# Two phases instead of one pipeline: the first product for every row and a store, then neighbour sums by accumulating gathers

## What is computed

```python
x = x + _L0_gnn_ref(_layernorm(x), edge_index, W, b)
x = x + _L0_ffn_ref(_layernorm(x)[None], ...)[0]
# _L0_gnn_ref, self edges added to the list (row, col):
h = jnp.einsum('nd,od->no', x, W) + b
deg = jnp.zeros((num_nodes,)).at[row].add(1.0)
deg_inv_sqrt = deg ** (-0.5)
norm = deg_inv_sqrt[row] * deg_inv_sqrt[col]
out = jax.ops.segment_sum(norm[:, None] * h[col], row, num_segments=num_nodes)
# _L0_ffn_ref: base product + shared rank 16 + 6 routed experts of rank 16, the best 2 weighted by a softmax
base_out = jnp.einsum('bsi,oi->bso', x, base_W) + base_b
```

## Time and profile before

| what | value |
|---|---|
| median of 3 runs | 2338.88 us (2337.76 to 2340.23) |
| span of the profiled execution | 2337.9 us |
| TensorE (PE) busy | 2259.6 us, 97% |
| VectorE (DVE) busy | 1602.0 us, 69% |
| ScalarE (ACT) busy | 399.7 us, 17% |
| GpSimd (POOL) busy | 410.7 us, 18% |
| moved by DMA | 113.56 MB, mean 49 GB/s |

### The profile page before, as it was taken

The page is one execution under the profiler, slowest core; times in us unless marked ns, Lnnn a source line. Parts: engine busy times, 40 slices in busy tenths (PEclk is TensorE's granted clock), DMA queues, the critical chain, the costliest instruction groups (busy, mean ns, idle before and its releaser), DMA issues.

```text
span 2337.9 us, 35957 instructions
## 1 busy us (share of the span) xinstructions
PE 2259.6 (97%) x12190; PEld 2060.8 (88%) x12190; DVE 1602.0 (69%) x4079; ACT 399.7 (17%) x808; POOL 410.7 (18%) x666
## 2 busy tenths in 40 slices
PE   3499999999999999999999999999999999999999
PEld 2389999999999999999999999999999999999998
DVE  8676676667667666667667766766666666676673
ACT  3011111121111111111111111111111111111110
POOL 9311111111111111111111111111111111111110
PEclk7699999999999999999999999999999999999999
DMA  4011111111111111111111111111111111111110
GB/s 188 17 44 46 44 47 50 43 44 45 47 51 53 46 45 45 44 45 46 54 45 45 45 46 49 51 46 44 45 44 44 44 55 46 46 45 44 48 38 27
DMA packets 39747, 113.56 MB, mean 49 GB/s; under 512 B 12138, under 2 KB 12217, under 8 KB 39730
## 3 DMA queue, kind: packets, MB, share of 16 engines
q1 hardware_dynamic: 25826, 92.79, 10.8%
q0 software_dynamic: 13904, 20.55, 3.3%
HBM read 92.78 MB, written 41.46 MB: 57 GB/s over the span
## 4 chain that ended last, share of the span: by engine, by line
PE 96%; DVE 3%; DMA 0%; issue 0%; ACT 0%; POOL 0%; POOLq 0%; SPq 0%; DVEq 0%
PE bo L616 15%; PE bo L618 14%; PE bo L617 14%; PE bg L616 13%; PE bg L618 13%; PE bg L617 13%; PE bt L625 6%; PE bo L698 2%; PE bo L702 2%; PE bo L700 2%; PE bt L663 2%; PE bt L664 2%; DVE slot_vals L770 1%; PE bm L665 0%; PE bm L691 0%; DVE hot_local L730 0%
## 5 line engine op out<-in xcount | busy, mean ns | idle before, releaser
L616 PE MATMUL bo<-base_hi,z_hi 128*128 128x380 f32 (+1 forms) x1896 | 659.3, 348 | 1.6 <-DVE z_lo L911 1.6
L618 PE MATMUL bo<-base_hi,z_lo 128*128 128x380 f32 (+1 forms) x1896 | 637.4, 336 | 0.0
L617 PE MATMUL bo<-base_lo,z_hi 128*128 128x380 f32 (+1 forms) x1896 | 635.9, 335 | 0.0
L616 PE MATMUL bg<-w_hi,u_hi 128*128 128x512 f32 x1264 | 507.1, 401 | 3.5 <-issue 2.0
L618 PE MATMUL bg<-w_hi,u_lo 128*128 128x512 f32 x1264 | 500.1, 396 | 0.0
L617 PE MATMUL bg<-w_lo,u_hi 128*128 128x512 f32 x1264 | 500.0, 396 | 0.0
L616 PEld LDWEIGHTS bo<-base_hi,z_hi 128*128 128x128 f32 x1896 | 357.5, 189 | 1.9 <-ACT z_hi L529 1.8
L617 PEld LDWEIGHTS bo<-base_lo,z_hi 128*128 128x128 f32 x1896 | 358.1, 189 | 0.0
L618 PEld LDWEIGHTS bo<-base_hi,z_lo 128*128 128x128 f32 x1896 | 356.0, 188 | 0.0
L922 DVE TENSOR_TENSOR y<-bo,y 128x262 f32<-128x262 f32 (+2 forms) x237 | 119.5, 513 | 320.6 <-PE bo L702 312.9
L467 POOL TENSOR_TENSOR pw<-pin,neg_half 128x4 f32<-128x4 f32 x79 | 80.6, 1021 | 1361.4 <-DVE pin L883 1337.8
(11 more groups left out here) (136 smaller groups left out, 2596.9 us busy)
## 6 DMA issues: line engine op xcount, KB each, us to landing
xb<-x SPq DMA_DIRECT2D x79, 512.0 KB, 4.4
out<-y SPq DMA_DIRECT2D x79, 512.0 KB, 2.6
base_raw<-base_t SPq DMA_DIRECT2D x8, 571.0 KB, 16.2
w_raw<-w_t SPq DMA_DIRECT2D x8, 512.0 KB, 6.8
xg<-x,row_now POOLq DMA_INDIRECT x79, 4.3
pin<-deg,row_now POOLq DMA_INDIRECT x79, 4.0
b_rows<-b SPq DMA_DIRECT2D x1, 512.0 KB, 11.4
bl_raw<-b_low SPq DMA_DIRECT2D x1, 452.0 KB
```

What stands on the lines that cost most here:

```text
L616: nc.tensor.matmul(ps, hi[:, k, :], m_hi[:, k, n], start=(k == 0), stop=False)
L617: nc.tensor.matmul(ps, hi[:, k, :], m_lo[:, k, n], start=False, stop=False)
L618: last = nc.tensor.matmul(ps, lo[:, k, :], m_hi[:, k, n], start=False, stop=(ends and k == KB - 1))
```

## The change

The kernel is cut into two phases, with a barrier between them.

Phase one, 79 steps written out without a loop: a tile of x is loaded (five buffers), normalised (`un`), transposed, multiplied by W (three pairs of banks), weighted by the node's deg^-0.5 on ScalarE (`weigh`), and b is added (`finish_rows`), which gives h; r = x * deg^0.5 + h. SP stores h and r to DRAM, 512 KB each. Nothing of the neighbours is needed here. Beside it, the edge tables are made: the one-hot tables in step 1 (`degrees`), 40 small products for the degrees in tile 2's product, the two powers for all 79 tiles at once on GpSimd in step 2, and in 28 of the steps from 6 on the rank of each edge among those of the same source (`compare`, up to 30 chunks of 128 comparisons in a step). From step 42 on GpSimd scatters the edges' targets into a slot table in DRAM, four slots for each node, which comes back in step 51. The dense layer's weights are loaded and split in steps 52 to 61, over the space of these tables. VectorE makes the low parts of the weights, where GpSimd did.

Between the phases GpSimd waits for every store of h and r and reads the overflow flag (a node with more than four outgoing edges); SP's loads of phase two wait for its signal.

Phase two, a loop of six steps a turn: SP loads a tile of r into one of six buffers `acc`; GpSimd adds to it, in four rounds, the rows h of the targets in slot 0, 1, 2 and 3, each by an indirect DMA that gathers and adds (`add_edges`). An empty slot points at one of 128 zero rows behind h, so every round moves 128 rows. The sum is the node's new row but for a factor deg^-0.5. VectorE takes its statistics (`acc_statistics`), ScalarE makes z, and the second product follows as before, with two sets of three banks. `finish` scales the sum and adds the product, and SP stores it. The gathered rows' normalisation, their split and the `sel` products are gone.

```diff
+ROUNDS = 4
+LANE_SLOTS = TILES * ROUNDS
+SLOTS = P * LANE_SLOTS
+DEEP = 6
+COMPARED = 30
+RANK_AT, SCATTER_AT, BASE_AT = 6, 42, 52
...
+                if s.has(-1):
+                    t = s.tile(-1)
+                    a = s.mod(-1, DEEP)
+                    sp.wait_ge(out_ok, 3 * (t + 1))
+                    sp.dma_start(out[rows(t), :], acc[a][:]).then_inc(out_stored[a], 16)
+                if s.has(5):
+                    a = s.mod(5, DEEP)
+                    if s.has(-1):
+                        sp.wait_ge(out_stored[a], 16 * (s.uses(5, DEEP) - 1))
+                    sp.dma_start(acc[a][:], r_dram[rows(s.tile(5)), :]).then_inc(r_in[a], 16)
+            sp.wait_ge(rows_ready, 1)
+            pipeline(sp, step, -5, TILES, 5)
...
+            def rstd(t):
+                pool.wait_ge(stats_ok, t + 1)
+                nc.gpsimd.tensor_tensor(pw[:], pin[:], neg_half[:, 0:1], ALU.pow) \
+                    .then_inc(rstd_ok, 1)
+            rstd(0)
+            rstd(1)
+            for t in range(TILES):
+                if t == 2:
+                    pool.wait_ge(deg_ok, 1)
+                    nc.gpsimd.tensor_tensor(dis[:], deg[:], neg_half[:], ALU.pow).then_inc(dis_ok, 1)
+                    nc.gpsimd.tensor_tensor(sqd[:], deg[:], pos_half[:], ALU.pow).then_inc(dis_ok, 1)
+                if t + 2 < TILES:
+                    rstd(t + 2)
...
+            def add_edges(a, q, r):
+                nc.gpsimd.indirect_dma_start(
+                    acc[a][:], None, h_dram,
+                    bass.IndirectOffsetOnAxis(ap=row_now[q][:, r:r + 1], axis=0),
+                    bounds_check=NPAD + P - 1, oob_is_err=True, compute_op=ALU.add) \
+                    .then_inc(added[r], 16)
             def step(s):
...
+                if s.has(4):
+                    t = s.tile(4)
+                    nc.gpsimd.tensor_copy(row_now[s.mod(4, 2)][:],
+                                          offs[:, bass.ds(t * ROUNDS, ROUNDS)]) \
+                        .then_inc(row_copied, 1)
+                    pool.wait_ge(row_copied, t + 1)
+                    pool.wait_ge(r_in[s.mod(4, DEEP)], 16 * s.uses(4, DEEP))
+                    carry_wait(4 + 4 * (s.q % 2))
+                    add_edges(s.mod(4, DEEP), s.mod(4, 2), 0)
+                if s.has(3):
+                    pool.wait_ge(added[1], 16 * (s.tile(3) + 1))
+                    carry_wait(5 + 4 * (s.q % 2))
+                    add_edges(s.mod(3, DEEP), s.mod(3, 2), 2)
                 if s.has(2):
...
+                    pool.wait_ge(acc_stats_ok, s.tile(2) + 1)
+                    nc.gpsimd.tensor_tensor(pw[:], pin[:], neg_half[:, 0:1], ALU.pow) \
+                        .then_inc(acc_rstd_ok, 1)
+                if s.has(4):
+                    pool.wait_ge(added[0], 16 * (s.tile(4) + 1))
+                    carry_wait(6 + 4 * (s.q % 2))
+                    add_edges(s.mod(4, DEEP), s.mod(4, 2), 1)
+                if s.has(3):
+                    pool.wait_ge(added[2], 16 * (s.tile(3) + 1))
+                    carry_wait(7 + 4 * (s.q % 2))
+                    add_edges(s.mod(3, DEEP), s.mod(3, 2), 3)
+                    pool.wait_ge(added[3], 16 * (s.tile(3) + 1))
+            pipeline(pool, step, -4, TILES - 3, 5)
...
+            def weigh(t):
+                if t == 0:
+                    act.wait_ge(dis_ok, 1)
+                if t >= 2:
+                    act.wait_ge(h_stored[t % 2], 16 * (t // 2))
+                    act.wait_ge(r_ok, t - 1)
+                for h in range(2):
+                    act.wait_ge(first_done, 2 * t + h + 1)
+                    nc.scalar.activation(hrow[t % 2][:, h * HALF:(h + 1) * HALF],
+                                         bg[t % 3][h][:], ACT.Copy, scale=dis[:, t:t + 1]) \
+                        .then_inc(h0_ok, 1)
...
+            for t in range(1, TILES):
+                pe.wait_ge(u_hi_ok, 2 * (t + 1))
+                pe.wait_ge(u_lo_ok, 2 * (t + 1))
+                for h in range(2):
+                    if t >= 3:
+                        pe.wait_ge(h0_ok, 2 * (t - 3) + h + 1)
+                    for k in range(KB):
+                        last = passes(bg[t % 3][h][:], u_hi[t % 2], u_lo[t % 2], w_hi, w_lo,
+                                      slice(h * HALF, (h + 1) * HALF), k, True)
+                    last.then_inc(first_done, 1)
+                    if h == 0 and t == 2:
+                        pe.wait_ge(hot_ok, 2)
+                        for c in range(CHUNKS):
+                            last = nc.tensor.matmul(bt[0][:, 0:TILES], hot_local[:, c, :],
+                                                    hot_tile[:, c, :], start=(c == 0),
+                                                    stop=(c == CHUNKS - 1))
+                        last.then_inc(deg_done, 1)
+                    if h == 0 and t + 1 < TILES:
+                        transpose_rows(t + 1)
...
-                    for h in range(2):
-                        half = slice(h * HALF, (h + 1) * HALF)
-                        nc.tensor.matmul(bt[h][:], sel[:], g_hi[:, half], start=True, stop=False)
-                        nc.tensor.matmul(bt[h][:], sel[:], g_lo[:, half], start=False, stop=True)
-                    nc.tensor.matmul(bm[:, HALF - 2:HALF - 1], sel[:].bitcast(F32), pw[:, 3:4],
-                                     start=True, stop=True).then_inc(sum_done, 1)
...
+            def finish_rows(t):
+                if t == 0:
+                    dve.wait_ge(rows_in, 32)
+                    dve.wait_ge(dis_ok, 2)
+                dve.wait_ge(h0_ok, 2 * (t + 1))
+                nc.vector.scalar_tensor_tensor(hrow[t % 2][:], b_rows[:], dis[:, t:t + 1],
+                                               hrow[t % 2][:], ALU.mult, ALU.add).then_inc(h_ok, 1)
+                dve.wait_ge(h_ok, t + 1)
+                nc.vector.scalar_tensor_tensor(xn[t % 5][:], xn[t % 5][:], sqd[:, t:t + 1],
+                                               hrow[t % 2][:], ALU.mult, ALU.add).then_inc(r_ok, 1)
...
+            def compare(pieces):
+                every = src_row[:].rearrange("q (p c) -> q c p", c=CHUNKS)
+                for c, a, to, where in pieces:
+                    first = CHUNKS - c + a
+                    link(nc.vector.scalar_tensor_tensor(
+                        same_src[:, 0:to - a, :], every[:, a:to, :], srcs[:, c:c + 1],
+                        earlier_of[:, first:first + to - a, :], ALU.is_equal, ALU.mult,
+                        accum_out=rank_parts[:, where, c:c + 1]))
...
+            for t in range(TILES + 1):
+                if t >= 3:
+                    finish_rows(t - 1)
+                if t + 2 < TILES and t != 2:
+                    statistics(t + 2)
+                if t == 1:
+                    degrees()
+                if t == 2:
+                    dve.wait_ge(deg_done, 1)
+                    nc.vector.tensor_scalar(deg[:], bt[0][:, 0:TILES], 1.0, None, ALU.add) \
+                        .then_inc(deg_ok, 1)
+                    dve.wait_ge(deg_ok, 1)
+                    link(nc.vector.reciprocal(dis2[:], deg[:]))
+                if t + 1 < TILES:
+                    low_rows(t + 1)
+                if t == 2:
+                    statistics(4)
+                if t + 2 < TILES:
+                    scales(t + 2)
+                if t == 2:
+                    finish_rows(0)
+                    finish_rows(1)
+                if t == RANK_AT - 1:
+                    columns()
+                if RANK_AT <= t < RANK_AT + len(PIECES):
+                    compare(PIECES[t - RANK_AT])
...
+            def acc_statistics(s):
+                n = s.tile(2)
+                a = acc[s.mod(2, DEEP)]
+                accs.start(n)
+                dve.wait_ge(added[3], 16 * (n + 1))
...
             def step(s):
-                if s.has(-2):
+                if s.has(-1):
                     finish(s)
-                if s.has(1):
-                    prepare_scales(s)
-                if s.has(-1):
-                    low_parts(s, -1, z_hi, z_lo, z_hi_ok, z_lo_ok)
-                if s.has(1):
-                    prepare_low(s)
+                if s.has(2):
+                    acc_statistics(s)
                 if s.has(0):
-                    dve.wait_ge(xb_ok, s.tile(0) + 1)
-                    make_y(s)
-                if s.has(1):
-                    if not s.has(0):
-                        dve.wait_ge(rows_in, 32)
-                    add_sum(s)
-                if s.has(0):
-                    make_z(s)
-                if s.has(-1):
                     choose(s)
                 if s.has(1):
-                    low_parts(s, 1, u_hi, u_lo, u_hi_ok, u_lo_ok)
-                if s.has(-1):
-                    p = s.tile(-1)
+                    low_parts(s)
+                if s.has(0):
+                    p = s.tile(0)
                     dve.wait_ge(hs_hi_ok, p + 1)
```

(89 more changed lines are left out.)

1038 lines of the change are left out of this document (472 added, 566 removed).

## The result

The change makes the kernel slower: 2623.38 us, median of 4 runs (2621.30 to 2625.43), against 2339.53 us for the kernel before on the same chip (4 runs, 2337.76 to 2340.23). The ratio is 1.122, 95% interval 1.120 to 1.123. The forecast was 2248 us, on the other side; the time lies at the upper end of the range, in the case called much slower gathers.

The account below looks back on a forecast made before the run. TensorE was taken to bound the kernel: 1000 for phase one, 51 between the phases, 2 for the clock, 79 x 15.06 (1190) for phase two and 4 at the end, 2247 us of span, 2248 us as median; range 2225 to 2635.

Parts of the forecast that it names:

- much slower gathers: Phase two: the chain of adding gathers sets the pace at 18 to 22 us a tile, 2480 to 2790 us; chance 0.27.
- The beginning: Start of phase one: constants, hot tables and powers delay TensorE; tile 4 starts at 96 us, 48 us late.
- one idle stretch of 15 us: Phase one, tile 3: TensorE idle behind GpSimd's two powers of 79 columns, named as a sign.
- a rival that came true: Phase one's 28 rank steps: VectorE bounds them, strided reads at slot_vals' rate, 36 us lost, 2284 us; within the 0.45.
- Between the phases: From phase one's end to TensorE's restart: 51 us with gathers of 4.5 us, 59 with 5.6, plus 2 for the clock.
- T = 3.95 + 2L: Phase two: time per tile of GpSimd's gather chain, with two landings L; TensorE's 15.06 us cover it up to L = 5.55.
- middle case: Phase two: adding costs one more read of 512 KB, L = 5.65, 15.3 us a tile, about 16.5 with collisions.
- The sign that I had named above all: Phase two: a landing of the gathers over 6 us would show the prediction wrong.
- my own sum: Whole kernel if gathers set the pace: 1000 + 37 first tile + 78 T + 38 last, so 1075 + 78 T.
- The two cases with slow gathers: Phase two paced by the gather chain: somewhat slower, 2290 to 2450 us, chance 0.28; much slower, 2480 to 2790, 0.27.
- the third: Phase two: TensorE stays the bound at 15.06 us a tile, 2248 us, own range 2225 to 2310; chance 0.45.
- the upper bound of L: Phase two: every byte new, 1.35 us for rows not moved now plus 2.7 for the added read; L 8.35, 20.7 us a tile.

Follow-up runs that it names:

- the experiment: The kernel after, with the row of sources stored once in comparison order so the rank operand is read without a stride: 2574.82 us, 48.6 us less.
- the two small cures: One power of 79 columns replaced by a VectorE product, and ranks read without a stride; with empty places skipped too, 2205.90 us, 0.944 of the kernel before.
- without the chain: The kernel after, with rounds 1 to 3 adding into buffers of their own and waited for a step later, their part of the sum left out: 2276.33 us.

## Why the prediction was wrong

**The beginning was right.** The order of waits came as walked through: hot tables in tile 1, the powers in tile 2, the power of tile 4 queued behind both. I had 12.3 us for each power and they took 12.99 and 12.97; the product of tile 4 started at 91.7 us where I had 96. In place of one idle stretch of 15 us TensorE had two, 7.24 us ahead of tile 3 and 6.11 us ahead of the transposes of tile 4. The first of them was not in the walk: tile 3 takes the banks of tile 0, which ScalarE's `weigh` empties only behind the first power.

**The ranks: a rival that came true.** I took the rate of the hot tables, 1.09 ns a column, over the 1.82 of `slot_vals`, because GpSimd had been at work beside the latter. For the ranks the operand's stride decides (2.10 against 1.15 ns, with GpSimd as idle in the one as in the other). The price put on that rival was 36 us; the experiment gave 48.6. Its name, strided reads at the rate of `slot_vals`, was wrong as well: `slot_vals` takes its wide operand in order, and what made it 1.82 ns no run shows. A view of the operand in the diff, `"q (p c) -> q c p"`, showed the stride; the question to ask was which row has one like it, and none had.

**Phase one without the ranks was right**: steps of 11.8 us (TensorE 399.45 of 400 us busy), 12.03 forecast. It ended at 1031 us instead of 1000: the ranks cost 53 us, and some 22 of these came back by the shorter steps and the earlier start. That the end was off by 31 only is in part luck.

**Between the phases**: 63 us from the last `weigh` to the first product of phase two, where I had 51 to 59 and 2 for the clock; by its own slope (8 us for 1.1 us of L) the same walk gives 68 with gathers of 6.9 us.

**The neighbour sums: the step that failed.** The form of the chain was right: I had T = 3.95 + 2L, and the timeline shows 2.97 + 0.7 + twice the time of a gather. The term that was mis-sized is L, the time of an adding gather from issue to landing, and with it fell the claim that TensorE's 15.06 us cover the chain. I took 4.3 to 5.5 us, near the plain gather of the earlier trace rows; the median landing is 6.9, and on the two places of the chain GpSimd gets to its next instruction 7.9 us after the issue. The runs split this:

- a plain gather of all 128 rows lands in 5.3 us, at the upper end of what I took. This alone would have left TensorE the bound, as the run without adding shows (2276.7 us);
- adding makes the issue 0.53 us longer (1.59 against 1.06, and the earlier trace rows had 1.09) and the engines' time 3.04 us instead of 1.64. My middle case had one more read of 1.35 us, a good size for the engines' time; for the landing the two together came to +1.6 us;
- the two places of the chain wait 1 us longer than the median landing (7.9 against 6.9); without SP's store it is 0.5 us (6.9 against 6.4). The rest is open. I had charged 1.2 us for collisions (16.5 against 15.3 us) in the middle case, and none in the one I chose; without the store the step is 1.9 us shorter.

The rule of the Trainium skill, page "Collectives: The Full Stack", section on SDMA and CCE, that the adding is free between two reads and a write, pointed to the middle case. The trace agrees with it for the engines' time: 3.04 against 1.64 us is 1.40 us more, about what SP's load or store of 512 KB takes (1.44 us), so that nothing shows up that the addition costs beside its read. The longer issue and landing are not in that rule. It should have moved my choice: of L's two ends I took the one whose row had no second read in it, though the destination must be read to be added to. The fit of the Trainium skill, page "DMA: Bandwidth & Descriptors", section on the anatomy of one DMA, is 2.0 us plus the bytes by 436 GB/s. The estimate by it of 3.2 us for 512 KB is far under the 5.3 us that the plain gather took beside the other transfers of this loop, and under its shortest of 4.2 us too.

The sign that I had named above all, a landing over 6 us, is in the page. With the measured step my own sum comes out: 1075 + 78 x 19.4 = 2588 us, and 31 us for the later end of phase one, 2619 us, against the span of 2623.6.

**The chances.** The two cases with slow gathers had 0.55 between them, and still I forecast the third, which had 0.45 as the largest single case. The much slower case, 18 to 22 us a tile, is what happened; the only thing that I held against it was that no row showed its price. A missing row is no such reason.

**What I didn't see: the bound.** I excluded that empty places are skipped, rightly, and priced the rows of zeros at 1.35 us, but only for the upper bound of L; what the kernel would take without them I never asked. By the draw the four rounds hold 5000 edges in 4 x 10112 places, so that seven eighths of the bytes are zeros (20.81 of 165.72 MB remain without them). Without them the whole loss is gone: with the bound moved, the change is worth 2.8%, and 5.6% with the two small cures. The same is true without the adding or without the chain, but this cure alone leaves the output as it is.

## What to carry to other kernels

Where transfers of one buffer must follow each other, price them by their time from issue to landing, once for each link, and compare the sum with the pace of the bounding engine: at 78% DMA load the chain cost 4.4 us a step, at 97% load without the chain nothing. For an adding gather of 512 KB take, by this case, 1.6 us more landing than for a plain one and nearly twice its engine time, and point padding outside the bound instead of at zero rows. Read in the diff how each new operand is strided before you take a rate for it from another instruction.

## What the runs showed of the hardware

- An adding indirect gather of 128 rows of 4 KB took 3.04 us of the 16 DMA engines (2.84 where they were at 97%), a plain one 1.64 us; median landing 6.9 us against 5.3 us, and 1.59 us against 1.06 us of GpSimd for the issue.
- Adding gathers of which seven eighths of the places are skipped landed in 2.9 us, but their issue took the same 1.59 us.
- VectorE's three-operand form read a float32 operand with 160 bytes between neighbours at 2.10 ns a column, and without a stride at 1.15 ns.
- A power on GpSimd took 12.99 us for 79 columns and 0.55 us for one, 0.16 us for each further column.
- While TensorE stopped for some 3 us a step of 19.4 us on average, its granted clock averaged 0.91 (the kernel after, 1200 to 2400 us); without these gaps it was 1.00 (empty places skipped, 1200 to 2100 us).
